# Routing logits added across partitions and turned in 32 x 32 squares by VectorE, in place of TensorE's transposes

## The reference, cut to what matters

```
h      = relu(((64 * x + sum over tokens of x) * relu(cond @ W3 + b3)) @ W2 + b2)     # 8192 tokens x 512
logits = h @ gate_w.T                                                                 # 8192 x 64 experts
scores = softmax(logits);  top 6 experts of each token
each expert takes its first 64 tokens:  y = (silu(h @ w_gate) * (h @ w_up)) @ w_down, weighted by the score
shared = (silu(h @ sw_gate) * (h @ sw_up)) @ sw_down                                  # all tokens, 704 wide
out    = x + sum of y over a token's experts + shared
```

## Time and profile before

| | |
|---|---|
| median of 3 runs | 1238.36 us (1238.19 to 1238.44) |
| profiled execution | 1238.84 us, of which its span (first to last instruction) is 1237.0 us |
| TensorE (PE) matmuls | 1223.1 us busy, 99% of the span, 5892 instructions |
| VectorE (DVE) | 741.7 us, 60%, 1405 instructions |
| ScalarE (ACT) | 333.2 us, 27% |
| GpSimd (POOL) | 272.4 us, 22% |
| mean granted clock of TensorE | 0.994 |

### The profile page before, as it was taken

One profiled execution on the slowest core, in us unless ns is written; L12 is line 12 of the kernel. 1 busy time (PEld: TensorE's weight loads), 2 busy tenths in 40 slices (PEclk: granted clock), 3 DMA queues, 4 the chain that ended last, 5 costly groups with the idle time before them and its releaser, 6 DMA issues.

```text
span 1237.0 us, 15789 instructions
## 1 busy us (share of the span) xinstructions
PE 1223.1 (99%) x5892; PEld 905.8 (73%) x5892; DVE 741.7 (60%) x1405; ACT 333.2 (27%) x632; POOL 272.4 (22%) x246
## 2 busy tenths in 40 slices
PE   8999999999999999999989999999999999999998
PEld 8888888888888888888756666666666666666666
DVE  6898989989888898877424234343333423423332
ACT  3654243434324443433111111110111201111110
POOL 0000000000000000000424355353552543545420
PEclk9999999999999999999989999999999999999999
DMA  9947444372644537058556987988979899899862
GB/s 185 232 121 189 96 132 115 90 183 48 182 94 126 122 90 181 16 152 282 158 191 234 329 270 262 350 265 277 337 233 321 302 273 300 284 286 309 273 144 78
DMA packets 159821, 250.91 MB, mean 203 GB/s; under 512 B 23616, under 2 KB 94400, under 8 KB 158592
## 3 DMA queue, kind: packets, MB, share of 16 engines
q1 hardware_dynamic: 143968, 223.66, 57.2%
q0 software_dynamic: 14048, 25.18, 10.0%
q10 hardware_dynamic: 1728, 1.05, 0.3%
HBM read 197.14 MB, written 61.10 MB: 209 GB/s over the span
## 4 chain that ended last, share of the span: by engine, by line
PE 93%; DVE 5%; issue 1%; DMA 1%; SPq 0%; ACT 0%; ACTq 0%
PE bank L1394 23%; PE bank L1396 22%; PE bank L1395 22%; PE bank L1594 12%; PE bank L1617 7%; PE bank L1513 1%; PE bank L1512 1%; PE bank L1450 1%; PE bank L1448 1%; PE bank L1603 1%; DMA x<-in_x_dram 1%; DVE x L882 1%; DVE xpart L886 1%; PE bank L1461 0%; DVE x L899 0%
## 5 line engine op out<-in xcount | busy, mean ns | idle before, releaser
L1394 PE MATMUL bank<-hh,gu 128*128 128x512 f32 x704 | 281.7, 400 | 3.0 <-issue 2.9
L1396 PE MATMUL bank<-hh,gu 128*128 128x512 f32 x704 | 275.7, 392 | 0.9 <-issue 0.8
L1395 PE MATMUL bank<-hl,gu 128*128 128x512 f32 x704 | 275.5, 391 | 0.9 <-issue 0.8
L590 POOL DMA_INDIRECT hg<-table,idx_quarter x128 | 127.1, 993 | 637.7 <-DVE idx_hi L1284 599.0
L1394 PEld LDWEIGHTS bank<-hh,gu 128*128 128x128 f32 x704 | 132.8, 189 | 40.1 <-issue 14.5
L1396 PEld LDWEIGHTS bank<-hh,gu 128*128 128x128 f32 x704 | 132.8, 189 | 30.0 <-issue 1.5
L1395 PEld LDWEIGHTS bank<-hl,gu 128*128 128x128 f32 x704 | 133.1, 189 | 29.3 <-issue 3.6
L650 ACT ACTIVATE ah<-prod 128x512 fp32r<-128x512 f32 x96 | 60.6, 632 | 303.1 <-DVE prod L949 285.7
L949 DVE TENSOR_TENSOR prod<-bank,prod 128x512 f32<-128x512 f32 x96 | 66.1, 688 | 125.4 <-PE bank L1396 108.8
L1394 PE MATMUL bank<-sdh,ah 128*128 128x512 f32 x320 | 126.8, 396 | 0.0
L1396 PE MATMUL bank<-sdh,al 128*128 128x512 f32 x320 | 124.7, 390 | 0.0
(11 more groups left out here) (128 smaller groups left out, 1676.5 us busy)
## 6 DMA issues: line engine op xcount, KB each, us to landing
wg<-in_L_ffn_w_gate_dram SPq DMA_DIRECT2D x64, 704.0 KB
wu<-in_L_ffn_w_up_dram SPq DMA_DIRECT2D x64, 704.0 KB
wd<-in_L_ffn_w_down_dram SPq DMA_DIRECT2D x64, 512.0 KB
table<-hrow SPq DMA_DIRECT2D x64, 256.0 KB, 4.3
x<-in_x_dram SPq DMA_DIRECT2D x60, 256.0 KB, 6.9
wd<-in_L_ffn_w_down_dram SPq DMA_DIRECT2D x64, 192.0 KB
out_dram<-outst SPq DMA_DIRECT2D x36, 256.0 KB
outst<-in_x_dram SPq DMA_DIRECT2D x32, 256.0 KB, 3.5
```

The source lines that it names most:

```text
L590: nc.gpsimd.indirect_dma_start(out=hg[p % 3][:, b, :], out_offset=None, in_=quarters, in_offset=bass.IndirectOffsetOnAxis(ap=idx_quarter[: ...
L1394: nc.tensor.matmul(o, st_h, mv_h, start=first_mm, stop=False)
L1395: nc.tensor.matmul(o, st_h, mv_l, start=False, stop=False)
L1396: return nc.tensor.matmul(o, st_l, mv_h, start=False, stop=last_mm)
```

## The change

TensorE's `logits(n)` is gone, for all 16 chunks, and with it ScalarE's `take_low(n)` and the waits on `logits_filled` and `z_ready`. ScalarE's `take_lraw` copies only the low half of the bank (64 partitions x 512) and signals `llow_ready`. A new VectorE function, `fold(n)`, adds high and low parts in eight instructions: each takes one of two groups of 32 experts (h) and one of four groups of 32-token columns (a) for all four 128-token pieces, and writes into partitions 32a to 32a + 31 of `lg`. Its last one counts `lraw_taken`. `route(n)` then transposes `lg` in 32 x 32 squares with one instruction in place of its add. The `fold` of chunk a stands behind `take_rows(c, 2)` of the round before (in round 0, `fold(0)` behind the first `split_h`, and `fold(2)` behind `take_down(0, 1)`), that of chunk b stands ahead of its `route`. The "rows" step comes one tile earlier, so VectorE turns the first pair's rows ahead of the second stage's first `product`, not behind it. The sync engine's wait before `load_gate(1)` is on `lraw_taken` in place of `logits_filled`.

```diff
-        lsb = keep("lsb", [P, CH])
+        lsb = keep("lsb", [E, CH])
...
-                    if v == ND and n == 1:
+                    if v == ND and n == 0:
                         yield "rows", 0, 0
...
-            sp.wait_ge(s.logits_filled, NCH)
+            sp.wait_ge(s.lraw_taken, NCH)
...
             def take_lraw(n):
                 act.wait_ge(s.lraw_filled, n + 1)
-                wait(act, s.logits_filled, n)
-                copy(lsb[:, :], lraw_bank(n)[:, :]).then_inc(s.lraw_taken, 1)
-
-            def take_low(n):
-
-                act.wait_ge(s.logits_filled, n + 1)
-                wait(act, s.z_ready, n)
-                parts = logits_bank(n)[:, :].rearrange("p (j h e) -> p h j e", j=J, h=2)
-                copy(lg[:, :, :], parts[:, 1, :, :]).then_inc(s.llow_ready, 1)
+                wait(act, s.lraw_taken, n)
+
+                copy(lsb[:, :], lraw_bank(n)[E:P, :]).then_inc(s.llow_ready, 1)
...
+            def fold(n):
+
+
+                dve.wait_ge(s.llow_ready, n + 1)
+                for a in range(P // SQ):
+                    for h in range(E // SQ):
+                        rows = slice(h * SQ, (h + 1) * SQ)
+                        full, low = (t[rows, :].rearrange("p (j a i) -> p a j i", j=J, i=SQ)[:, a, :, :]
+                                     for t in (lraw_bank(n), lsb))
+                        op = nc.vector.tensor_tensor(lg[a * SQ:(a + 1) * SQ, :, rows], full, low, ALU.add)
+                op.then_inc(s.lraw_taken, 1)
+
             def route(n):
-
-                parts = logits_bank(n)[:, :].rearrange("p (j h e) -> p h j e", j=J, h=2)
-                dve.wait_ge(s.llow_ready, n + 1)
-                link(nc.vector.tensor_tensor(lg[:, :, :], parts[:, 0, :, :], lg[:, :, :], ALU.add))
+                dve.wait_ge(s.lraw_taken, n + 1)
+                squares = lg[:, :, :].rearrange("p j e -> p (j e)")
+                link(nc.vector.transpose(squares, squares))
...
                     split_h(b, oc)
+                    if i == 0 and oc == 0:
+                        fold(a)
...
+                    fold(b)
                     route(b)
                     product(v, 0)
...
                     take_rows(c, 2)
+                    fold(c)
                     merge_drop(*m[6])
...
                 product(v, 4)
+                fold(b)
                 route(b)
                 mark(b)
...
                 take_down(v, 1)
+                fold(c)
                 take_down(v, 2)
...
-                if oc == 2:
-                    pe.wait_ge(s.z_ready, n if n % 2 == 0 else n - 1)
...
-            def logits(n):
-                pe.wait_ge(s.lraw_taken, n + 1)
...
-                for j in range(J):
-                    op = nc.tensor.transpose(logits_bank(n)[:, j * P:(j + 1) * P], lsb[:, j * P:(j + 1) * P],
-                                             ident[:, :])
-                op.then_inc(s.logits_filled, 1)
```

More of the change, by code:

```diff
@@ L234, in adaln_moe_ffn_kernel @@
             lraw_taken = sem("lraw_taken")
-            logits_filled = sem("logits_filled")
             llow_ready = sem("llow_ready")
@@ L350, in lraw_bank @@
             return bank[7 if n == 0 else 5]
-        def logits_bank(n):
-            return bank[7] if n == 0 else bank[3] if n % 2 == 0 else bank[6]
         def second_stage():
@@ L776, in body @@
                     take_cond(b, oc)
-                    if i > 0 and oc == 0:
-                        take_low(a)
                     if i > 0 and oc == 2:
@@ L792, in body @@
                 silu(v, 0)
-                if i > 0:
-                    take_low(b)
                 split_a(v, 0)
@@ L1552, in body @@
                 if i > 0:
-                    cond_tile(b, 0)
-                    logits(a)
-                    for oc in range(1, KC):
+                    for oc in range(KC):
                         cond_tile(b, oc)
                     down_tile(v - 1, 3)
-                else:
-                    logits(a)
                 logits_raw(b)
@@ L1562, in body @@
                     gu_tile(v, t)
-                    if t == (2 if i == 0 else 0):
-                        logits(b)
                     if i > 0 and t == (5 if more else 2):
```

## The result

The changed kernel takes 1252.46 us (median of 5 runs, 1250.32 to 1253.51); the kernel before, beside it, 1238.19. The ratio is 1.0116, 95% interval 1.0105 to 1.0127: 1.2% slower, 14 us, where 1.2 us less was predicted. The profiled execution, the fastest of the five, took 1250.32 us, with a span of 1248.5.

What follows compares the result with a forecast made beforehand. TensorE's issue was taken to pace steady rounds, with VectorE also a bound in round 0. The terms -6.6 + 3.4 + 0.9 + 1.6 - 0.5 = -1.2 us on the median 1238.36 gave 1237.1 us, range 1232.0 to 1241.8.

Steps and rivals of the forecast that it cites:

- TensorE's gain: From chunk 2 on, fourteen transpose groups of 0.47 us leave TensorE's path: 6.6 us less.
- What fold costs: On VectorE, eight adds 0.295 us apart plus 0.08 of lost overlap: 2.44 us, bounds 1.7 and 3.4.
- the second kind of pair: VectorE copies at 589.18: the next reads from another first partition and starts 0.20 later, once the first is done.
- overlap: Rival: fold's steps on VectorE overlap, 0.20 apart, fold 1.7 us; total -4.9, 1233.4 us; chance 0.18.
- a costlier add: Rival: VectorE's adds into other partitions take 0.42 us each, fold 3.4; total +7.7, 1246 us; chance 0.13.
- Round 0: VectorE's folds make TensorE 3.4 us late at logits_raw(2), and fold(2) 0.9 more at cond_tile(3, 1).
- Rounds 1 to 3, and none from round 4: TensorE's small waits for late VectorE work sum to 1.6 us; from round 4 VectorE's 10 us slack leaves none.
- the second leg: Not forecast; found after: VectorE's work from take_down back to take_rows(c, 3), 52.85 us before, 54.2 in the changed kernel.
- the ring: Not forecast; found after: take_rows(c, 3), sync engine's queue, load_xr, take_down, VectorE's work back to rows; 73.3 us a round.
- The rows step: Ahead of the first expert matmul, VectorE's rows transpose moves into idle time: -0.5 us, bounds -0.67 and 0.
- The slow stretch: Rival: at 618 to 633 us TensorE's 9.5 us loss changes: 1232.3 or 1241.9 us; chance 0.12, either way alike.
- The clock at the new wait: Rival: near 97 us TensorE's clock falls at the 3.4 us wait; over 10.3 us costs about 4: 1241; chance 0.07.

Runs made afterwards that it cites:

- the sync order: Changed kernel with store_out(i - 1, 2) and load_xr(i - 1, 3) ahead of load_x(d) on the sync engine: ratio 0.9984 to kernel before; repeated, 0.9981.
- `fold(c)` behind the rows: Changed kernel with fold(c) moved behind take_rows(c, 3) in rounds 1 to 6: ratio 1.0006 to the kernel before.
- the transposes kept: Changed kernel with four transposes of a constant where each group stood in rounds 1 to 7: ratio 1.0113 to the kernel before.
- Round 0's order: Changed kernel with the sync order, plus chunk 2's splits ahead of chunk 3's work in round 0 on ScalarE and VectorE: ratio 0.9982 to kernel before.

## Why the prediction was wrong, step by step

**TensorE's gain: right.** Two groups a round were put at 0.94 us. Rounds without a wait take 71.19, 0.96 less than 72.15, in the runs with the sync order or with `fold(c)` behind the rows. The estimate of 0.22 us a group, worked out from the Trainium skill (VectorE: DVE Perf Modes, the cost table in its section on the TRN2 errata), is not borne out by these 0.48.

**What fold costs: right.** 2.44 us were predicted; the changed kernel shows the first one and the two groups:

```profile
45.12 2.35 DVE L975 TENSOR_TENSOR lg<-bank,lsb 32x128 f32<-32x128 f32 x8
...
L975 DVE TENSOR_TENSOR lg<-bank,lsb 32x128 f32<-32x128 f32 x128 | 35.7, 279 | 1.5
L981 DVE STREAM_TRANSPOSE lg<-lg 128x256 f32<-128x256 f32 x16 | 7.1, 442 | 0.3
```

279 ns each, eight in 2.35: starts 0.295 apart, the second kind of pair, none overlapping. The rivals of overlap (0.20) and of a costlier add (0.35 and more) fall with it. The transposes take 0.02 us more than the old adds did. By the rule of the Trainium skill (VectorE: DVE Perf Modes, "Two Vector instructions with no wait between them") each add is held until the one before has finished, and this trace agrees.

**Round 0: right.** The last matmul of `logits_raw(2)` was put at 100.6 and stands at 100.72. The wait before `cond_tile(3, 1)` was put at 0.9 and was 0.7:

```profile
112.37 0.50 PE L1396 MATMUL bank<-xmh,w2h 128*128 128x512 f32 x1 [0.70 <-DVE lg L975]
```

At chunk 5 the prediction's terms give 3.4 + 0.9, less three groups of 0.47, plus 0.35 for two small waits, 3.2 us, and it was 3.1. (Its own 2.8 belongs to product(2, 1), one group later, and by then four groups are gone, not five as it says.)

**Rounds 1 to 3, and none from round 4: the step that failed.** The term was 1.6 us. From chunk 5 to chunk 15 the changed kernel fell back by 7.3 us (10.45 - 3.12) while five rounds of TensorE's gain, 4.8, should have brought it forward: 12.1 us lost in rounds 2 to 6, of which the profile lists 7.6 as idle time before a matmul, and 1.0 more at `ranksT(7)`, for which no term stood:

```profile
574.99 0.66 PE L1479 MATMUL bank<-ident,ranks 128*128 128x128 f32 x4 [0.95 <-DVE ranks L1000]
```

The sentence at fault is "From round 4 VectorE has 10 us of slack, against 4.9 of folds: none." The 10 us were the engine's idle time in a round, but 1.7 of the idle time before stood in front of `take_down`, waiting for a transfer that VectorE's own earlier work had released, and 3.05 stood before the routing of chunk 10, waiting for ScalarE, in the same leg; only the 4.5 us of the second leg could have taken up a fold, and 1.5 of those stayed. Idle time in a leg of the ring that runs over DMA can't take up work put in the other leg. The same for "`product`, and the splits" as the list of what is queued behind `fold`: behind `fold(c)` stood `take_rows(c, 3)` too, with a queue of eleven DMA issues and VectorE's own `take_down` behind it. What is queued behind `fold`, and who waits for that, was asked for TensorE alone. Runs that show it: the sync order (the same work of VectorE and TensorE, 14 to 16 us less) and the transposes kept (more work, same time). Between the forecast's -1.2 and the 11.5 of the trace lie 12.7 us: 12.1 - 1.6 are these rounds, 1.0 is `ranksT(7)`, 1.0 is the slow stretch below.

**The rows step: right in its place, lost in the sum.** -0.5 was put, 0.58 is in the trace.

**The slow stretch: as a rival, weak.** From the first expert matmul to the transposes behind the stretch it was 18.2 us before and 20.3 after, 2.1 of the 11.5 us at most, and 1.1 came back later. (In the prediction's chances this rival is said to go either way alike, 0.06 each; the sums appear to use 0.07 and 0.05.) **The clock at the new wait** did not fall in the changed kernel (granted clock 1.00 from 100.4 to 104.5 us). In the first run with the new sync order it did, once, behind the same wait:

```profile
101.00:106.40 5.40, 5.40 (x17) 0.71 0.30 96
```

(TensorE's busy time, then the clock.) Sixteen steps between matmuls took 4.9 us there in place of 3.65: the first ones 0.43 us each, which is the level of 0.50 (1.2 GHz), the later ones 0.23. TensorE had been busy for 2.36 of the 4 us before. The run repeated had the same waits and 1.00 at this place.

## What to carry to other kernels

Slack is a property of a ring, not of an engine: before work is added to an engine with idle time, follow what the instruction behind it releases, over DMA queues and back to the same engine, add up the legs, and compare that sum with the period of the bounding engine. A wait for a transfer in front of an instruction of a busy engine (1.7 us in the trace before, a row that was there to see) was here the sign that such a ring was nearly closed. And a queue of DMA issues is part of it: the cheapest cure was to put two issues ahead of four others, and the one with the lowest ratio was to give the work to an engine outside the ring.

## What the runs showed of the hardware

- **The slow stretch at 618 to 633 us goes with the chip.** On the chips where the kernel before took 1229.4 us, six kernels went from the first expert matmul to the transposes of the first pair in 10.46 to 10.49 us, at a granted clock of 1.00. Where it took 1237.9 to 1239.1 us, eight kernels took 17.6 to 21.7 us for the same instructions, with a granted clock of 0.71 to 0.79 there (0.79 in the kernel before, 0.71 in the changed one, 0.74 in "Round 0's order"). No kernel has a trace on both kinds of chip, but the kernel before itself is some 9 us faster on the first kind. With 4 us of spread half a microsecond can't be resolved there. What sets the stretch off stays open.
- **The sync engine's issue of the same DMA differs with what stands ahead of it:** `store_out` of 256 KB took 2.87 us right behind the four issues of `load_x`, and 0.58 right behind `keep_x`. With the new order `store_scores` is the one behind `load_x`, and takes 2.81 us in place of 0.45. So 3.5 us of `load_x` and 2.3 of `store_out` left the ring; the wait of 1.7 us for a transfer came in, and 4.0 were gained.
- **GpSimd adds 32 x 128 elements from SBUF in 0.45 us at best**, starts 0.51 apart (in six chunks 0.59 to 0.64, in the first two 0.98 and 0.71), against VectorE's 0.28 with one input in PSUM and starts 0.295 apart. Of VectorE's groups between 170 and 540 us the one that grew most beside it, `xml` in split_xm, took 1.249 us in place of 1.211.
